# Cross attention's transposed scores in six banks per tile instead of eight

## The reference, cut to what matters

```python
q = (Q @ w_q.T).reshape(B, S, G, HG, HD)      # S = 128 tokens, G = 8 groups, HG = 4 heads, HD = 8
k = (K @ w_k.T).reshape(B, S, G, HD)
v = (V @ w_v.T).reshape(B, S, G, HD)
scores = jnp.einsum('bnghd,bmgd->bnghm', q, k) / scale
scores = jnp.where(pad, NEG_INF, scores)
causal = jnp.tril(jnp.ones((S, S), bool))[None, :, None, None, :]
scores = jnp.where(causal, scores, NEG_INF)
attn = jax.nn.softmax(scores, axis=-1)
out = jnp.einsum('bnghm,bmgd->bnghd', attn, v).reshape(B, S, D)
```

## Time and profile before

| | |
|---|---|
| median of 3 runs | 672.81 us |
| lowest, highest | 668.51, 675.12 us |
| the profiled execution | 668.76 us, of it the core's span 667.0 us |
| TensorE busy | 559.1 us (84%) |
| VectorE busy | 409.5 us (61%) |
| ScalarE busy | 353.0 us (53%) |
| GpSimd busy | 325.9 us (49%) |

### The profile page before, as it was taken

One profiled execution on the slowest core, in us unless ns is written; L12 is line 12 of the kernel. 1 busy time (PEld: TensorE's weight loads), 2 busy tenths in 40 slices (PEclk: granted clock), 3 DMA queues, 4 the chain that ended last, 5 costly groups with the idle time before them and its releaser, 6 DMA issues.

```text
span 667.0 us, 13267 instructions
## 1 busy us (share of the span) xinstructions
PE 559.1 (84%) x3141; PEld 427.6 (64%) x3141; DVE 409.5 (61%) x1932; ACT 353.0 (53%) x853; POOL 325.9 (49%) x468
## 2 busy tenths in 40 slices
PE   2699999999999999999783499788988889898970
PEld 1476766677676667766452377676777777676750
DVE  1456677778777777875475245344554446776795
ACT  2356767776676767666640135344554545544440
POOL 3202165555656555665516535355555555564560
PEclk9989999999999999999986689899999999998895
DMA  6320245522122121211104457666644558888855
GB/s 213 126 64 22 99 168 158 153 77 73 67 82 73 59 68 65 81 67 67 57 13 128 158 172 231 203 193 191 179 129 118 158 151 280 284 277 250 263 158 198
DMA packets 50587, 92.96 MB, mean 139 GB/s; under 512 B 9830, under 2 KB 39182, under 8 KB 50322
## 3 DMA queue, kind: packets, MB, share of 16 engines
q1 hardware_dynamic: 34482, 43.73, 22.8%
q0 software_dynamic: 12288, 32.15, 13.4%
q10 hardware_dynamic: 3744, 16.24, 7.7%
HBM read 52.72 MB, written 43.54 MB: 144 GB/s over the span
## 4 chain that ended last, share of the span: by engine, by line
PE 60%; issue 10%; ACT 8%; SPq 7%; DVE 5%; DMA 4%; another core or an unknown queue 3%; POOL 2%; POOLq 0%; ACTq 0%; DVEq 0%
PE bank L1233 10%; PE bank L1259 7%; PE bank L1098 5%; PE bank L1079 5%; PE bank L1112 4%; PE bank L1099 4%; ACT KA L486 4%; PE bank L1080 4%; PE bank L970 4%; PE bank L1050 3%; PE bank L1211 3%; ACT Q L414 2%; PE bank L965 2%; SPq L307 2%
## 5 line engine op out<-in xcount | busy, mean ns | idle before, releaser
L406 POOL DMA_INDIRECT parts<-PT,dst x108 | 108.0, 1000 | 97.4 <-ACT PT L414 58.0
L396 POOL DMA_INDIRECT rows<-rowb,idx x112 | 110.5, 987 | 72.8 <-DVE rowb L783 39.2
L1233 PE MATMUL bank<-wgu_sb,PT 128*128 x576 | 130.8, 352 | 8.8 <-issue 7.2
L1233 PEld LDWEIGHTS bank<-wgu_sb,PT 128*128 128x128 f32 x576 | 95.1, 199 | 24.9 <-issue 23.7
L414 ACT ACTIVATE PT<-bank 128x512 f32<-128x512 f32 x126 | 71.9, 596 | 63.1 <-PE bank L1259 31.3
L1259 PE MATMUL bank<-wd_sb,VC 96*128 x288 | 78.9, 397 | 10.8 <-ACT VC L414 7.4
L501 ACT ACTIVATE PT<-bank,padcol 128x512 f32<-128x512 f32 x128 | 78.7, 707 | 15.0 <-PE bank L1099 15.0
L683 DVE TENSOR_REDUCE NM<-bank 128x4 f32<-128x512 f32 x128 | 80.5, 686 | 8.5 <-PE bank L1080 8.4
L905 DVE SCALAR_TENSOR_TENSOR PT<-PT,bank 128x192 f32<-128x192 f32 x72 | 25.4, 353 | 98.1 <-ACT PT L541 63.2
L1259 PEld LDWEIGHTS bank<-wd_sb,VC 96*128 96x128 f32 x288 | 52.6, 195 | 22.1 <-issue 17.4
L1098 PE MATMUL bank<-Q,KA 128*128 128x512 f32 x128 | 55.5, 434 | 12.9 <-ACT Q L414 12.0
(11 more groups left out here) (229 smaller groups left out, 1062.2 us busy)
## 6 DMA issues: line engine op xcount, KB each, us to landing
pool_a<-rows SPq DMA_DIRECT2D x144, 148.5 KB
wgu_sb<-wgu_d SPq DMA_DIRECT2D x8, 768.0 KB
pool_a<-parts ACTq DMA_DIRECT2D x5, 896.0 KB
KA<-parts ACTq DMA_DIRECT2D x5, 896.0 KB
Q<-parts ACTq DMA_DIRECT2D x4, 896.0 KB
rows<-pad SPq DMA_DIRECT2D x23, 152.0 KB, 1.8
wd_sb<-wd_d SPq DMA_DIRECT2D x2, 1536.0 KB
pool_a<-x_d SPq DMA_DIRECT2D x16, 128.0 KB, 2.0
```

Of the source, the lines that this page charges most:

```text
L396: gp.indirect_dma_start(out=rows, out_offset=bass.IndirectOffsetOnAxis(ap=idx[b % 2][:, k:k + 1], axis=0), in_=rowb[b % 2][:, :], in_offse ...
L406: gp.indirect_dma_start(out=parts, out_offset=bass.IndirectOffsetOnAxis(ap=dst[q % FEED][:, j:j + 1], axis=0), in_=yb[q % FEED][:, j, :], ...
L1233: last = t.matmul(GU_PS[q % 2][:, j * 2 * NI:(j + 1) * 2 * NI], xTb[q % 2][:, j, k * P:(k + 1) * P], wgu_sb[:, k, one_of(expert[i]), :].sq ...
```

## The change

A bank of `s` no longer holds one group. Per half of the heads (`hf`, four groups) there are three banks instead of four:

- kinds 0 and 1: two groups each, all 128 keys x (4 heads x the 64 later queries) of each group;
- kind 2: the 64 earlier queries of four groups. Only the 64 earlier keys matter here, so two groups share the partitions: `KL` holds the first 64 key columns of every group, group 2i on partitions 0 to 63 and group 2i+1 on 64 to 127.

Each bank gets the causal mask first (512 columns, now with `start=True`) and then two products of 256 columns. `pv` becomes four 32-column products over the later queries and two 64-column products over the earlier ones; for the latter `vaL` holds the values of the earlier 64 keys twice, on partitions 0 to 63 for even groups and on 64 to 127 for odd ones. The second copy comes from a further product in `kv`, whose output is on partitions 64 to 127. A new GpSimd step `kL` copies `KL` out of `KA`. The offsets of the remaining steps stay as they are; `s6` and `s7` go.

```diff
-           ... "s5": 36.4, "s6": 37.3, "s7": 37.9, "pv0": 38.4, ...            (PE)
+           ... "s5": 36.4, "pv0": 38.4, ...
-           ... "s5": 37.6, "s6": 38.9, "s7": 39.6, "pv0": 40.3, ...            (ACT)
+           ... "s5": 37.6, "pv0": 40.3, ...
-    "POOL": {"r1": -14.9, ...
+    "POOL": {"kL": 19.5, "r1": -14.9, ...
+        causLr = sb("causLr", [P, H], f32r)
-        mcol = sb("mcol", [P, NB], i32)
+        mcol = sb("mcol", [P, 2 * NB], i32)
+        KL = sb("KL", [P, NG * H], f32r)
+        vaL = [PT[:, 6, 2 * p:2 * p + 2, :].rearrange("p h n -> p (h n)") for p in range(2)]
-                    small("mcol", (mcol[:, :], maskT))
+                    small("mcol", (mcol[:, 0:NB], maskT), (mcol[0:H, NB:], maskT[0:H, :]), (mcol[H:P, NB:], maskT[0:H, :]))
...
+                gp.memset(vaL[p][:, :], 0.0).then_inc(S["vl"], 1)
+                pool.wait_ge(S["vl"], 3 * p + 1)
+                for u in range(2):
+                    gp.memset(vaL[p][u * H:u * H + H, :].rearrange("p (n c) -> p n c", c=H)[:, :, 32 * u + HD:32 * u + HD + 1], 1.0).then_inc(S["vl"], 1)
+                    pool.wait_ge(S["vl"], 3 * p + 2 + u)
...
+            def kL(b):
+                pool.wait_ge(S["KA"], nth("KA", b))
+                if b == 0:
+                    pool.wait_ge(S["sel"], 2)
+                else:
+                    pool.wait_ge(S["s"], nth("s", b - 1, 6))
+                gp.tensor_copy(KL[:, :].rearrange("p (g m) -> p g m", g=NG), KA[b % 2][:, :, 0:H]).then_inc(S["kl"], 1)
...
-                copy(va_g[b % 2][:, :, 0:HD], o[:, GD:2 * GD].rearrange("p (g d) -> p g d", g=NG)).then_inc(S["va"], 1)
+                copy(va_g[b % 2][:, :, 0:HD], o[:, GD:2 * GD].rearrange("p (g d) -> p g d", g=NG))
+                if b == 0:
+                    act.wait_ge(S["vl"], 6)
+                for u in range(2):
+                    last = copy(vaL[b % 2][u * H:u * H + H, :].rearrange("p (n c) -> p n c", c=H)[:, :, 32 * u:32 * u + HD],
+                                o[u * H:u * H + H, (1 + u) * GD:(2 + u) * GD].rearrange("p (n two d) -> p n two d", two=2, d=HD)[:, :, u, :])
+                last.then_inc(S["va"], 1)
...
                 for k in range(KC):
                     last = t.matmul(o[:, 0:2 * GD], ctx_sb[b % 2][:, k, :], wkv_sb[:, k, :], start=k == 0, stop=k == KC - 1)
+                for k in range(KC):
+                    last = t.matmul(o[H:P, 2 * GD:3 * GD], ctx_sb[b % 2][:, k, 0:H], wkv_sb[:, k, GD:], start=k == 0, stop=k == KC - 1)
                 last.then_inc(S["kv"], 1)
...
-                    t.matmul(o[:, :], KA[b % 2][:, g, :], Q2[b % 2][:, g // HG, :, :].rearrange("p h n -> p (h n)"), start=True, stop=False)
-                    t.matmul(o[:, :].rearrange("p (h n) -> p h n", h=HG), nident[:, :], causTr[:, :].unsqueeze(1).to_broadcast([P, HG, P]),
-                             start=False, stop=True).then_inc(S["s"], 1)
+                    if i == 2:
+                        pe.wait_ge(S["kl"], nth("kl", b))
+                    later = causTr[:, H:] if kind < 2 else causLr[:, :]
+                    t.matmul(o[:, :].rearrange("p (a n) -> p a n", n=H), nident[:, :], later.unsqueeze(1).to_broadcast([P, 2 * HG, H]),
+                             start=True, stop=False)
+                    for u in range(2):
+                        if kind < 2:
+                            keys, queries = KA[b % 2][:, HG * hf + 2 * kind + u, :], Q2[b % 2][:, hf, :, H:]
+                        else:
+                            keys, queries = KL[:, P * (2 * hf + u):P * (2 * hf + u + 1)], Q2[b % 2][:, hf, :, 0:H]
+                        last = t.matmul(o[:, 2 * P * u:2 * P * (u + 1)].rearrange("p (h n) -> p h n", h=HG), keys, queries, start=False, stop=u == 1)
+                    last.then_inc(S["s"], 1)
...
                     for k in range(4):
-                        g = 4 * n + k
-                        last = t.matmul(V_PS[32 * k:32 * k + 32, :], va[b % 2][:, g * (HD + 1):g * (HD + 1) + 32],
-                                        PT[:, g, :, :].rearrange("p h n -> p (h n)"), start=True, stop=True)
+                        g, flat_p = 4 * n + k, PT[:, 3 * n + k // 2, :, :].rearrange("p h n -> p (h n)")
+                        t.matmul(out4[32 * k:32 * k + 32, :, H:], va[b % 2][:, g * (HD + 1):g * (HD + 1) + 32],
+                                 flat_p[:, 2 * P * (k % 2):2 * P * (k % 2 + 1)].rearrange("p (h n) -> p h n", h=HG), start=True, stop=True)
+                    flat_p = PT[:, 3 * n + 2, :, :].rearrange("p h n -> p (h n)")
+                    for u in range(2):
+                        last = t.matmul(out4[H * u:H * u + H, :, 0:H], vaL[b % 2][:, H * (2 * n + u):H * (2 * n + u + 1)],
+                                        flat_p[:, 2 * P * u:2 * P * (u + 1)].rearrange("p (h n) -> p h n", h=HG), start=True, stop=True)
                     last.then_inc(S["pv"], 1)
```

More of the change, by code:

```diff
@@ L17 @@
 KEEP = 0.8
+H = 64
 NTOK = NB * P
@@ L63 @@
 READ = {"kv": ("klo", 1), "kT": ("KA", 1), **{f"mx{u}": ("rmax", u + 1) for u in range(8)}, "c": ("Q3c", 1),
-        **{f"s{g}": ("e", g + 1) for g in range(NG)}, **{f"vt{n}": ("on", n + 1) for n in range(2)},
+        **{f"s{i}": ("e", i + 1) for i in range(6)}, **{f"vt{n}": ("on", n + 1) for n in range(2)},
         "oT": ("oT2_sb", 1), "wo": ("x2", 1), "xT": ("xT_sb", 1), "lg": ("eall", 1), "rk": ("pt", 1),
@@ L177, in decoder_kernel @@
         kjnk, ksl, dst = sb("kjnk", [P, 4, TOP]), two("ksl", [P, 2]), [sb(f"dst{n}", [P, 2], i32) for n in range(FEED)]
-        wjnk, wsl = sb("wjnk", [P, 4, NE]), two("wsl", [P, 2])
+        wjnk, wsl = con[:, 3 * P:3 * P + 4 * NE].rearrange("p (a e) -> p a e", a=4), two("wsl", [P, 2])
         th, av, hv = ([u.rearrange("p (j n) -> p j n", j=2) for u in shared(2 * NI)] for _ in range(3))
@@ L197, in ring_bank @@
             return RING[TURN[use, b] % NRING]
-        PER = dict(Q2=2, qT=2, mx=8, rmax=8, s=8, e=8, pv=2, vc=2, vt=2, rdx=2, on=2, cu=4, gu=2, keep=2, mr1=2, e8=2, fsum=4)
+        PER = dict(Q2=2, qT=2, mx=8, rmax=8, s=6, e=6, pv=2, vc=2, vt=2, rdx=2, on=2, cu=4, gu=2, keep=2, mr1=2, e8=2, fsum=4)
         names = ("w_first w_small w_bias w_more w_con wgu wd mcol setup_v setup_g setup_p wc wback zw "
@@ L398, in sc @@
                 return f
-            schedule("POOL", {"r1": r1, "r4": r4, "r7": r7, "r13": r13, "r17": r17, "wo": wo_, "xT": xT, **{f"sc{k}": sc(k) for k in range(SENT)}})
+            schedule("POOL", {"kL": kL, "r1": r1, "r4": r4, "r7": r7, "r13": r13, "r17": r17, "wo": wo_, "xT": xT, **{f"sc{k}": sc(k) for k in range(SENT)}})
             for q in range(NPAIR):
@@ L527, in _ @@
             schedule("ACT", {"mk": mk, "r3": r3, "r7": r7, "r8": r8, "r10": r10, "r11": r11, "r12": r12, "r15": r15, "r16": r16, "r17": q_rows(0), "r17b": q_rows(1),
-                      "kv": kv, "kT": kT, "c": c, **{f"s{g}": s_(g) for g in range(NG)}, "pv0": pv(0), "pv1": pv(1),
+                      "kv": kv, "kT": kT, "c": c, **{f"s{i}": s_(i) for i in range(6)}, "pv0": pv(0), "pv1": pv(1),
                       "oT": oT_, "xT": xT, "g1": g1})
@@ L599, in mi @@
                 v.tensor_copy(causalr[:, :], causal).then_inc(S["setup_v"], 1)
-                v.tensor_copy(causTr[:, :], causalT).then_inc(S["setup_v"], 1)
+                v.tensor_copy(causTr[:, :], causalT)
+                v.tensor_copy(causLr[0:H, :], causalT[0:H, 0:H])
+                v.tensor_copy(causLr[H:P, :], causalT[H:P, H:P]).then_inc(S["setup_v"], 1)
             def mk(_):
-                dve.wait_ge(S["mcol"], 16)
+                dve.wait_ge(S["mcol"], 3 * 16)
                 v.tensor_scalar(padcol[:, :], mcol[:, :], 0.0, -BIG, ALU.is_equal, ALU.mult).then_inc(S["pc"], 1)
@@ L1089, in c, with s_ @@
                 last.then_inc(S["cT"], 1)
-            def s_(g):
+            def s_(i):
+                hf, kind = i // 3, i % 3
                 def f(b):
-                    o = ring(f"s{g}", b)
-                    if g == 0:
+                    o = ring(f"s{i}", b)
+                    if i == 0:
                         pe.wait_ge(S["Q3c"], nth("Q3c", b))
@@ L1179, in _ @@
                       "r17": q_half(0), "r17b": q_half(1), "kv": kv, "kT": kT, **{f"mx{u}": mx(u) for u in range(8)}, "c": c,
-                      **{f"s{g}": s_(g) for g in range(NG)}, "pv0": pv(0), "pv1": pv(1), "vt0": vt(0), "vt1": vt(1), "oT": oT_, "wo": wo_,
+                      **{f"s{i}": s_(i) for i in range(6)}, "pv0": pv(0), "pv1": pv(1), "vt0": vt(0), "vt1": vt(1), "oT": oT_, "wo": wo_,
                       "xT": xT, "lg": lg, "rk": rk_})
```

26 lines of the change are left out of this document (14 added, 12 removed), and 10 rows, old and new, of tables (AT, names).

## The result

| | median | lowest to highest | against before, 95% interval |
|---|---|---|---|
| before (15 runs beside it) | 675.12 us | 668.51 to 681.97 us | |
| changed (15 runs) | 682.68 us | 677.14 to 687.94 us | 1.0109, 1.0083 to 1.0136 |
| the changed kernel's profiled execution | 686.12 us, span 684.3 us | | |

The change makes the kernel slower by 1.1%, 7.6 us. Forecast were 674.5 us, with a range of 667 to 682, and, with a chance of 0.70, a change too small to be told from none; the result lies outside the range and on the side that had a chance of 0.22.

The account below looks back on a forecast made before the run. TensorE was taken to bound the first stage. Periods +1.4 and start +0.94 make +2.3 us: 671.1 on the profiled execution, 675.1 on the median, written as 674.5 us, range 667 to 682.

Parts of the forecast that it names:

- The steady part: Middle tiles of the first stage: scores -0.53, `pv1` +0.13, `kv` product +0.50, so +0.10 us per period, some 14 periods.
- Products 0.117 apart: Scores on TensorE: a 256-column product costs by its columns, 0.117 us, saving 0.94 us per tile.
- A wait of `r16` for ScalarE: After `pv0`: `r16` waits about 0.3 us for ScalarE's copy `r15`, so 0.53 of 0.94 us saved gets through.
- The prediction's slack: At `pv0`: 0.41 us of the scores' saving held up behind `r16`, of which `pv0` uses its added 0.13.
- `pv1` +0.15, forecast +0.13: Value products: a 0.09 us gap for the width change and longer first weights, 0.13 us more; 0.05 without the gap.
- the term for the start: Start of the first stage: two more `mcol` loads issued ahead of tile 1's input delay everything by 0.94 us.
- price nothing, cover gone at 0.3: ScalarE's two small copies in `kv`: VectorE's `kv` starts 0.3 us later but idles afterwards, so no cost.
- the page's row of the granted clock: First stage: clock at or near full, 2.4 GHz, so matmul durations need no correction.
- The strips of 64 do run side by side: Rival that they don't: `pv1` +0.43 us, period +0.68, sum +10.4, 683 us; chance 0.12.
- GpSimd did not become the wait: Rival that it does: `kL` takes 1.3 us, `r8` waits 0.3, period +0.40, sum +6.5, 679 us; chance 0.12.
- TensorE's saving did not come whole: Rival that it does: ScalarE doesn't hold `r16`, narrow products are cheap, period -0.59, total -7.3 us; chance 0.08.
- The forecast's case: Whole kernel: +2.3 us, from +1.4 over the periods and +0.94 at the start, own range -2 to +6; chance 0.51.

Follow-up runs that it names:

- e9: Changed kernel with the copies of `xT` and `r15` one exponential earlier; 679.39 us, ratio 0.9915 to the changed kernel run beside it, period 19.37.
- e5: The changed kernel itself, measured once more on the second chip: 632.97 us, ratio 1.0070 to the kernel before.
- e6: Kernel before with only the buffer `wjnk` moved into the tile `con`, on the second chip: 628.58 us, ratio 1.0000.
- e10: Changed kernel with the lower half of the value products as four 32-column strips instead of two of 64: 680.69 us, ratio 1.0035 to before.
- e7: Changed kernel without the further `kv` product (ScalarE copies across partitions) and with the two further `mcol` loads issued late; second chip: 624.04 us, ratio 0.9914 to before.
- e8: Kernel before plus the further `kv` product and ScalarE's two copies, unused, with the new buffer places; second chip: 640.41 us, ratio 1.0157.
- e1: Kernel before with its buffers at the changed kernel's places, same instructions: 675.66 us, ratio 1.0035.
- e2: Kernel before with three loads of `mcol` instead of one: 675.75 us, ratio 0.9988.
- e11: Changed kernel with `kv` product replaced by ScalarE copies, two `mcol` loads late, 32-column strips throughout, `xT` and `r15` copies earlier: 669.22 us, ratio 0.9901 to before.

## Why the prediction failed

**The steady part was right.** Products 0.117 apart: yes. `pv0` starts 3.53 after `s0`, 4.45 before: 0.92 earlier, forecast 0.94. A wait of `r16` for ScalarE: yes. The profile shows 0.17 of idle time, counted from the recorded end of `pv0`; by the starts it is 0.25, since `r16` follows `pv0` after 207.65 - 206.25 = 1.40 where `pv1` takes 1.15. The prediction's slack, 0.41 - 0.13 = 0.28, is of that kind, and e9 gets 0.23 back. `pv1` +0.15, forecast +0.13. `kv` +0.47 in the changed kernel (0.92 against 0.45), forecast +0.50. `kL` 0.62, the estimate was 0.8, and `r8` doesn't wait. Period 19.60, forecast 19.6. On the second chip (e5 against e6) the twelve periods from tile 1 to tile 13 are 1.15 us longer together, which is 0.10 each. From there to the second stage's first down product e5 is 0.6 shorter, so the end of the stage gains a little, where the prediction had nothing.

The Trainium skill's rule (TensorEngine Tiling (Array Packing), Key Properties) that a change of the tiling mode drains TensorE is borne out for this pair too: the second pass starts 0.12 us later when the width changes (e10), which no row of before showed. What TensorE does in the gap no row tells.

**The step that failed is the term for the start: +0.94 forecast, +3.0 measured at `mx0`.** The prediction had one thing in it, the loads. It counted the product in `kv` for the 14 periods alone, and at the clock's upper level, and said of ScalarE's copies "price nothing, cover gone at 0.3" and of `kL` that it lies beside other work. Both were read from a tile in the middle, where the engines have work of several tiles. In the first two tiles the engines have little else to do, and TensorE, ScalarE, VectorE and GpSimd stand in one chain, each waiting for the one before. What the change puts into it came through in full, twice where both tiles pass it. The chain in the second chip's traces, e6 (as before) and then e5 (changed), VectorE in time:

```profile
16.65 0.43 DVE L589 BATCH_NORM_STATS2 st_ln<-pool_a 128x6 f32<-128x256 f32 x1 [5.08 <-DMA pool_a<-x_d]
...
20.02 0.23 DVE L670 TENSOR_TENSOR kN<-bank,kN 128x64 fp32r<-128x64 f32 x1 [0.75 <-ACT va L414]
...
26.95 0.41 DVE L594 TENSOR_SCALAR pool_a<-pool_a,mv_ln,scalars 128x256 f32<-128x256 f32 x1 [0.74 <-POOL scalars L355]
```

```profile
17.32 0.43 DVE L611 BATCH_NORM_STATS2 st_ln<-pool_a 128x6 f32<-128x256 f32 x1 [5.44 <-DMA pool_a<-x_d]
...
21.57 0.23 DVE L694 TENSOR_TENSOR kN<-bank,kN 128x64 fp32r<-128x64 f32 x1 [1.64 <-ACT PT L429]
...
28.50 0.68 DVE L616 TENSOR_SCALAR pool_a<-pool_a,mv_ln,scalars 128x256 f32<-128x256 f32 x1 [0.74 <-POOL scalars L362]
```

TensorE around `kv` of tile 1, e6 and then e5, and GpSimd's `kL` in e5:

```profile
33.41 1.06 PE L1060 MATMUL bank<-wkv_sb,ctx_sb 128*128 128x128 f32 x4
34.26 1.06 PE L1050 MATMUL bank<-con,qN 128*96 128x128 f32 x4
```

```profile
35.22 1.06 PE L1084 MATMUL bank<-wkv_sb,ctx_sb 128*128 128x128 f32 x4
...
36.83 0.69 PE L1074 MATMUL bank<-con,qN 128*96 128x128 f32 x4
```

```profile
28.42 0.61 POOL L384 CAST KL<-KA 128x512 fp32r<-128x512 f32 x1
```

- Loads: 17.32 - 16.65 = 0.67 (1.08 on the first chip).
- `kv`'s product and ScalarE's copies for tile 0: from the input to VectorE's `kN` 4.25 us against 3.37, +0.88. 0.28 of that are the copies: in e7, which has them and not the product, VectorE waits 1.03 where e6 has 0.75. The rest, 0.60, is the product, at the clock's lower level.
- `kL`: the normalisation of `x` takes 0.68, not 0.41, +0.27, while GpSimd's copy runs from 28.42 to 29.03. In e8, without `kL`, it takes 0.41; in all nine traces of kernels with `kL` it takes 0.67 or 0.68.
- `kv`'s product for tile 1, at the lower level again: 36.83 - 35.22 = 1.61 from `kv` to the next start in e5, against 34.26 - 33.41 = 0.85 in e6, +0.76.

Together 2.58. `mx0` moves by 2.20, because in e5 the clock rose at 37.1 and the rest of the way to `mx0` went at the upper level. In the pair of before and changed the same terms, read from its own traces, are 1.08, 0.88, 0.26 and 0.76, together 2.98, and `mx0` moved by 2.99. e8, which has the product and the copies alone, checks two of them: 0.88 + 0.76, less 0.32 for its earlier input, is 1.32, and its `mx0` moved by 1.35.

The prediction also read the page's row of the granted clock as full speed from the start of the stage on. The row says so, but the matmuls up to 37.7 us of the kernel before last as they do at the lower level, and so the product cost 0.60 and 0.76 in the first two tiles, and not the 0.47 of the middle.

On SBUF's shared port, the Trainium skill (SBUF — State Buffer, Who interferes with whom) has it that, where VectorE runs in a two-port mode, which `tensor_scalar` can enter, it and GpSimd contend, and whichever issues first keeps the shared ports for its whole instruction while the other is blocked. The row fits that: GpSimd's copy started first, at 28.42, and ended at 29.03, and VectorE's instruction ended 0.15 after it. Whether VectorE was in that mode, and whether it stood still or was slowed, no row tells.

**The level was mis-set by 2.3 us.** The forecast stood on a median of three runs, 672.81; fifteen runs of the same kernel have 675.12. Of the 8.2 us between 674.5 and 682.68, this is 2.3, rounding the sum of 675.1 down to 674.5 is 0.6, and the change itself, +7.6 and not +2.3, is 5.3; of those the start explains 2.1 and the rest is the open part below.

**What stays open.** The start (3.0 on the first chip), the periods (1.2) and the last tiles (-0.6), these two from the second chip, make 3.6 us. Measured were +7.6 there (some 2 us to each side), +4.2 on the second chip and, on the third, +5.3 by the medians or +7.5 by the ratio (some 4 us to each side). So the second and, barely, the third are explained within their uncertainty, and on the first 4 us, half of the change, are left. Between the two traces of the second chip the last 1.1 of the span's 3.9 us arise in the second stage, which is the same in both. On the other two chips that stage has most of the waits put down to an unknown queue, and the last tiles go otherwise than on the second chip. There the last two distances between `c` are 18.7 to 19.5 and 18.1 to 18.4 us in the four traces; on the other two chips all ten traces take 20.6 us or more for each, with TensorE standing ahead of the maxima for no reason that the profile shows. In the three traces with the instructions of before (before, e1, e2) the long one, 22.9 to 24.7, is the last; in the seven of the changed family it is mostly the last but one, up to 25.0. From `c` of tile 13 to the first down product the three take 87.1, 89.0 and 90.6 us and the seven 89.4 to 92.6. The gain of 0.6 isn't seen there, and a loss of some 2 us is possible, but three traces that differ by 3.5 among themselves don't show it. Whether the changed kernel meets more of these waits and stands, what they are, and whether the places of the buffers matter on such a chip (e1 leaves room for 0.7%, e6 has `wjnk` alone at nothing on the second chip) isn't settled.

**The rivals.** None came true. The strips of 64 do run side by side (210.58 - 210.00 = 0.58 for a pass, as against 0.57 for one of 32), GpSimd did not become the wait, and TensorE's saving did not come whole, for the reason given: ScalarE held `r16`. The forecast's case itself, "+2.3, own range -2 to +6", holds the second chip's +4.2, but not the +7.6, and of the third's two readings only the +5.3.

**What the kernel would have to be.** The change saves 0.94 us per tile on TensorE and pays 0.47 for a second copy of 64 rows that ScalarE can write from the first, 0.15 at each of two places for a change of width (at `pv0` of the changed kernel `r16`'s wait hides it), and 0.23 for the place of one copy. With those taken away (e11) the period falls by 0.88, nearly the whole 0.94, and the kernel is 1.0% faster than before.

## What to carry to other kernels

Price an added step twice: in the steady tile, where it may hide, and in the first tile or two, where the same step lies in a bare chain, at the clock level of that stretch; "price nothing" holds for the first only. When a change frees time on the bounding engine, list at once who held the next instruction and who stands behind it: here a quarter of the saving (0.23 of 0.94) stood behind one small copy's place in another engine's list. And where a product has left a value in PSUM on the wrong partitions, try copying it across before computing it again: here the copy cost ScalarE no more than the one it replaced, and TensorE was spared 0.47 us per tile.
